# Attention with wider value slots, a ring of 18, a short opening, and the causal mask of the row maxima on VectorE

## The reference

```
scores = einsum('bihd,bjhd->bhij', q, k) * SCALE      # 32 heads, four to a key head
scores = where(causal, scores, finfo.min)
attn = softmax(scores, axis=-1)
out = einsum('bhij,bjhd->bihd', attn, v)
x = layernorm(x + out.reshape(b, s, 1024) @ wo)
```

## Time and profile before

| | us |
|---|---|
| median of 3 runs (3942.48 to 3944.07) | 3943.87 |
| the profiled execution | 3945.43 |
| its span, first to last instruction | 3943.6 |
| PE busy | 3616.7 (92%) |
| VectorE busy | 2041.4 (52%) |
| POOL busy | 1863.9 (47%) |
| ScalarE busy | 1429.3 (36%) |

### The profile page before, as it was taken

The page is one execution under the profiler, slowest core; times in us unless marked ns, Lnnn a source line. Parts: engine busy times, 40 slices in busy tenths (PEclk is TensorE's granted clock), DMA queues, the critical chain, the costliest instruction groups (busy, mean ns, idle before and its releaser), DMA issues. The chain is left out here.

```text
span 3943.6 us, 73049 instructions
## 1 busy us (share of the span) xinstructions
PE 3616.7 (92%) x25741; PEld 2464.1 (62%) x25741; DVE 2041.4 (52%) x3597; ACT 1429.3 (36%) x1821; POOL 1863.9 (47%) x807
## 2 busy tenths in 40 slices
PE   8999989999999989999999999999839999999975
PEld 7888875555555555555555555555428888888851
DVE  3121227566666666666666665666234444443448
ACT  2111103455555555555555554555521111110114
POOL 0000003887797798788789778878910000000000
PEclk9999997999999999999999999999969999999989
DMA  5333333111111111111111111110043232223237
GB/s 187 109 107 121 106 101 82 39 30 45 45 29 48 45 31 36 47 43 26 45 45 31 45 44 36 33 30 10 7 145 87 72 83 80 78 77 80 69 114 248
DMA packets 222653, 269.69 MB, mean 68 GB/s; under 512 B 59608, under 2 KB 145112, under 8 KB 222328
## 3 DMA queue, kind: packets, MB, share of 16 engines
q1 hardware_dynamic: 222328, 265.50, 23.2%
HBM read 167.38 MB, written 97.52 MB: 67 GB/s over the span
## 5 line engine op out<-in xcount | busy, mean ns | idle before, releaser
L716 DVE TENSOR_REDUCE p_part_max<-p_qm 128x1 f32<-128x512 f32 (+3 forms) x2240 | 1411.3, 671 | 792.9 <-PE p_qm L565 543.6
L535 POOL TENSOR_TENSOR p_psums<-p_psums,p_probs 128x1024 f32<-128x1024 f32 x672 | 1595.6, 2374 | 123.7 <-ACT p_probs L675 74.0
L675 ACT ACTIVATE p_probs<-p_km 128x1024 f32<-128x1024 f32 x1024 | 1008.7, 1022 | 770.6 <-PE p_km L589 516.2
L565 PE MATMUL p_qm<-p_k_st,p_q_st 96*128 96x512 f32 (+3 forms) x2560 | 984.9, 432 | 11.1 <-DMA p_q_st<-q_hi 10.7
L589 PE MATMUL p_km<-p_q_st,p_k_st 97*128 97x512 f32 x2048 | 709.1, 426 | 24.7 <-issue 24.7
L32 POOL MEMSET p_ident<- 128x128 f32 x4 | 0.8, 204 | 1511.8 <-POOLq L791 929.8
L565 PEld LDWEIGHTS p_qm<-p_k_st,p_q_st 96*128 96x128 f32 x2560 | 484.6, 200 | 300.3 <-DVE p_part_max L716 164.7
L599 PE MATMUL p_o<-p_probs,p_v 128*32 128x256 f32 (+1 forms) x9216 | 630.5, 382 | 0.2 <-ACT p_probs L672 0.2
L589 PEld LDWEIGHTS p_km<-p_q_st,p_k_st 97*128 97x128 f32 x2048 | 385.4, 199 | 100.1 <-issue 31.5
L599 PEld LDWEIGHTS p_o<-p_probs,p_v 128*32 128x32 f32 x9216 | 244.6, 111 | 269.3 <-issue 144.9
L531 POOL TENSOR_TENSOR p_psums<-p_probs 128x1024 f32<-128x1024 f32 x112 | 266.0, 2375 | 309.9 <-ACT p_probs L675 308.3
(11 more groups left out here) (153 smaller groups left out, 3699.7 us busy)
## 6 DMA issues: line engine op xcount, KB each, us to landing
p_q_st<-q_hi SPq DMA_DIRECT2D x128, 256.0 KB, 4.8
p_x_raw<-in_L_attn_x SPq DMA_DIRECT2D x8, 2048.0 KB, 8.4
q_hi<-p_out_hi SPq DMA_DIRECT2D x64, 256.0 KB, 2.0
q_lo<-p_out_lo SPq DMA_DIRECT2D x64, 256.0 KB, 2.3
p_q_st<-q_lo SPq DMA_DIRECT2D x64, 256.0 KB, 4.4
attended_T<-p_o_raw SPq DMA_DIRECT2D x128, 128.0 KB
p_a_raw<-attended_T SPq DMA_DIRECT2D x32, 512.0 KB, 4.3
p_recip<-reciprocals SPq DMA_DIRECT2D x128, 128.0 KB, 5.9
```

What stands on the lines that cost most here:

```text
L535: pool.tensor_tensor(sums[:, :, :], sums[:, :, :], probs[s % PB][:, :, :], ALU.add).then_inc(added, 1)
L565: last = pe.matmul(bank[:, x * keys:(x + 1) * keys], q_st[par][0:ROWS, c, h + x, sub * P:(sub + 1) * P], k_st[par][0:ROWS, j * CK:j * CK + ...
L675: act.activation(probs[s % PB][:, :, :].rearrange("p h q -> p (h q)"), km[s % 2][:, :, :].rearrange("p a b -> p (a b)"), ACT.Exp, scale=SC ...
L716: dve.reduce_max(part_max[c][:, h:h + heads, sub, j], qm[bank_of(i)][:, 0:item_width(i)].rearrange("p (h k) -> p h k", h=heads), AX.X).the ...
```

## The change

Five edits in `attend`.

1. The values of up to five steps are done together. `SLOTS` cuts each chunk's 2c + 2 steps into equal parts of at most five: 2; 4; 3, 3; 4, 4; 5, 5; 4, 4, 4; 5, 5, 4; and 4, 4, 4, 4. That is 18 slots a group. PE does all scores of a slot, with their items between them, then the values of the slot before. No item is placed behind values any more.
2. The ring `probs` has 18 tiles instead of 12.
3. `POOLED` is 2c - 1 for c > 1 and 0 for chunks 0 and 1.
4. The mask matmuls of the items are gone. For a diagonal item VectorE runs one `tensor_tensor_reduce` per head: it adds `mask_q` (now fp32, 512 wide, zero but for its last 128 columns) to the bank in place and takes the maximum into `part_max`. Ahead of the first stands a semaphore increment, which takes the wait.
5. Ahead of group 0 only items 0 to 15 are done. The other items of group 0, and those it does for group 1, are placed by `OPENING`: 28 in steps 0 to 3, 44 in steps 4 to 17, 56 in steps 18 to 39, 72 in steps 40 to 71. From then on `STEADY` places two a step, and the last group's `CLOSING` its own items only.

```diff
-    PB = 12
+    MOST = 5
+    SLOTS = []
+    for c in range(NC):
+        n = 2 * c + 2
+        parts = -(-n // MOST)
+        cuts = [FIRST_STEP[c] + (n * i + parts - 1) // parts for i in range(parts + 1)]
+        SLOTS += [(c, list(range(a, b))) for a, b in zip(cuts, cuts[1:])]
+    PB = 18
-    POOLED = [2 * c for c in range(NC)]
+    POOLED = [2 * c - 1 if c > 1 else 0 for c in range(NC)]
...
+    ROW_AT = [ITEMS.index(("maxrow", c)) for c in range(NK)]
+    FIRST_AHEAD = ROW_AT[0] + 1
+    STEADY = place([(0, AHEAD), (NS, NI + AHEAD)])
+    OPENING = place([(0, FIRST_AHEAD)] + [(FIRST_STEP[2 * c] - 2, ROW_AT[c] + 1) for c in range(1, NK)]
+                    + [(NS, NI + AHEAD)])
+    CLOSING = [[(ahead, i) for ahead, i in items if not ahead] for items in STEADY]
...
-        mask_q = sb("p2_mask_q", [P, P], BF16)
+        mask_q = sb("p2_mask_q", [P, CK], F32)
...
                 for x in range(item_heads(i)):
                     last = pe.matmul(bank[:, x * keys:(x + 1) * keys], q_st[par][0:ROWS, c, h + x, sub * P:(sub + 1) * P],
-                                     k_st[par][0:ROWS, j * CK:j * CK + keys], start=True, stop=j < c)
-                    if j == c:
-                        last = pe.matmul(bank[:, (x + 1) * keys - P:(x + 1) * keys], ident_bf[:, :], mask_q[:, :],
-                                         start=False, stop=True)
+                                     k_st[par][0:ROWS, j * CK:j * CK + keys], start=True, stop=True)
...
+            def group(n, par, placed):
+                for sl, (_, steps) in enumerate(SLOTS):
+                    for s in steps:
                         scores(n, par, s)
+                        for ahead, i in placed[s]:
+                            item(n + ahead, (par + ahead) % 2, i)
+                    if sl > 0:
+                        values(n, par, sl - 1)
...
-                dve.reduce_max(part_max[c][:, h:h + heads, sub, j], qm[bank_of(i)][:, 0:item_width(i)].rearrange(
-                    "p (h k) -> p h k", h=heads), AX.X).then_inc(item_read, 1)
+                if j < c:
+                    dve.reduce_max(part_max[c][:, h:h + 1, sub, j], qm[bank_of(i)][:, :], AX.X).then_inc(item_read, 1)
+                else:
+                    hold()
+                    keys = item_keys(i)
+                    for x in range(heads):
+                        part = qm[bank_of(i)][:, x * keys:(x + 1) * keys]
+                        last = dve.tensor_tensor_reduce(
+                            part, part, mask_q[:, CK - keys:CK], 1.0, LOWEST, ALU.add, ALU.max, part_max[c][:, h + x, sub, j:j + 1])
+                    last.then_inc(item_read, 1)
```

More of the change, by code:

```diff
@@ L289, in offset @@
         return P if t == 2 * c + 1 else 0
-    POOLED = [2 * c for c in range(NC)]
+    POOLED = [2 * c - 1 if c > 1 else 0 for c in range(NC)]
+    POOL_CHUNKS = [sum(m > 0 for m in POOLED[:c]) for c in range(NC + 1)]
     ADDS_BEFORE = [sum(max(0, m - 1) for m in POOLED[:c]) for c in range(NC + 1)]
@@ L303, in attend @@
     TLAG = 4
+    LOWEST = -3e38
     def key_tiles(c, sub, j):
@@ L349, in attend, with row_steps @@
     bank_user = lambda i: i - QM if i >= QM else max(x for x in range(NI) if x % QM == i) - NI
+    def row_steps(placed):
+        return [(s, ahead, ITEMS[i][1]) for s, items in enumerate(placed) for ahead, i in items
+                if ITEMS[i][0] == "maxrow"]
     def at_least(engine, semaphore, value):
@@ L441, in store_o, with group @@
                              ).then_inc(o_stored[c % 2], 16)
-            def group(n, par, last=False, load=True):
+            def group(n, par, placed, load=True, more=True):
                 b, g = batch_head(n)
@@ L616, in values @@
                 last.then_inc(slot_done, 1)
-                if t == 2 * c + 1 and c > 0:
+                if t == 2 * c + 1 and POOLED[c]:
                     pe.wait_ge(added, n * NADD + ADDS_BEFORE[c + 1])
                     weighted(ones[:, :], psums[c % 2], CQ, 0, False).then_inc(chunk_done, 1)
-            def group(n, par, last=False):
-                done = 0
-                for k, (part, s, _) in enumerate(PARTS):
-                    if part == "scores":
+            def group(n, par, placed):
+                for sl, (_, steps) in enumerate(SLOTS):
+                    for s in steps:
                         scores(n, par, s)
-                    elif s >= 0:
-                        values(n, par, s)
+                        for ahead, i in placed[s]:
+                            item(n + ahead, (par + ahead) % 2, i)
+                    if sl > 0:
+                        values(n, par, sl - 1)
                     elif not (isinstance(n, int) and n == 0):
                         values(n - 1, 1 - par, NSL - 1)
-                    for i in ROUND[done:ITEMS_BY[k]]:
-                        if i >= AHEAD:
-                            item(n, par, i)
-                        elif not last:
-                            item(n + 1, 1 - par, i)
-                    done = ITEMS_BY[k]
             pe.wait_ge(ident_done, 2)
             pe.wait_ge(consts_done, 6)
-            for i in range(AHEAD):
+            for i in range(FIRST_AHEAD):
                 item(0, 0, i)
-            group(0, 0)
+            group(0, 0, OPENING)
             with pe.Fori(0, NG // 2 - 1) as i:
-                group(2 * i + 1, 1)
-                group(2 * i + 2, 0)
-            group(NG - 1, 1, last=True)
+                group(2 * i + 1, 1, STEADY)
+                group(2 * i + 2, 0, STEADY)
+            group(NG - 1, 1, CLOSING)
             values(NG - 1, 1, NSL - 1)
@@ L708, in _, with hold @@
         def _(dve):
+            def hold():
+                dve.sem_inc(held, 1)
             def item(m, i):
@@ L720, in item, with group @@
                     dve.reduce_max(row_max[c][:, :], part_max[c][:, :, :, :].rearrange("p h s j -> p (h s) j"), AX.X).then_inc(max_done, 1)
-            def group(n, last=False):
-                for i in ROUND:
-                    if i >= AHEAD:
-                        item(n, i)
-                    elif not last:
-                        item(n + 1, i)
+            def group(n, placed):
+                for items in placed:
+                    for ahead, i in items:
+                        item(n + ahead, i)
+            dve.wait_ge(consts_done, 4)
             for i in range(2):
                 dve.memset(k_st[i][ROWS:ROWS + 1, :].bitcast(F32), 1.0).then_inc(consts_done, 1)
-            for i in range(AHEAD):
+            for i in range(FIRST_AHEAD):
                 item(0, i)
-            group(0)
+            group(0, OPENING)
             with dve.Fori(0, NG // 2 - 1) as i:
-                group(2 * i + 1)
-                group(2 * i + 2)
-            group(NG - 1, last=True)
+                group(2 * i + 1, STEADY)
+                group(2 * i + 2, STEADY)
+            group(NG - 1, CLOSING)
 class Chain:
```

115 lines of the change are left out of this document (50 added, 65 removed).

## The result

| | us |
|---|---|
| before, median of 3 runs | 3943.87 |
| changed, median of 3 runs (3843.30 to 3849.85) | 3846.84 |
| ratio, with its 95% interval | 0.9755 (0.9732 to 0.9777) |
| the profiled execution (also 3846.84), its span | 3845.1 |
| forecast | 3834 (3775 to 3965) |

The change takes 97 us off. That is the predicted direction, and 13 us above the forecast. First the page of the changed kernel: PE's share and the new instruction of VectorE (count | busy, mean ns of one | idle before).

A forecast was written before the change was run, and what follows sets the result against it. PE was taken to bound groups 1 to 14, VectorE the opening, POOL the last group's second half. Savings of 95 (fourteen groups), 15 (last group) and 0 (opening), 110 us, gave 3835.4, as median 3834 us (3775 to 3965).

The forecast's parts named there:

- Masks off TensorE: PE, each group: removing 64 mask matmuls, sixteen for each width, saves 5.4 us.
- Fewer slots and VectorE: Each group: 36 slots become 18, 4.1 us less; PE waiting for VectorE's reads in scores phases, 9.5 us more.
- the formula: Scores phase of n steps: last item starts at 1.71 + (2n - 4) x 0.61 us, values 0.33 later.
- POOL: Each group: 6.6 us waiting goes except 0.9, 4.1 of clock returns; more steps of ones on PE add 3.0.
- The masked read: VectorE's add-and-maximum instruction: 0.28, 0.41, 0.54, 0.68 us by width, including 0.08 for writing its maximum out.
- rival 3: VectorE becomes the bound, masked reads at half rate: 4039 us; chance 0.13 for beyond 3965.
- The cost of a dearer read: Groups: a dearer masked read delays PE in 90 of 144 places; 0.1 us more per read costs 4.0 us.
- The opening: Before and in group 0: PE starts about 617.7, group 0 takes 154 us, ends at 771.7; net nothing, bounds 12.
- The last group: Paced by POOL's adds in its second half: 130 us against 146, charged as 15 us less.
- Rival 1: The masked read's maximum comes out free and POOL never waits: 3764 us; chance 0.13 for under 3790.
- Rivals 2: The masked read acts as a dear pair, 0.17 us more each, 6.8 a group: 3941 us; chance 0.24 (3885 to 3965).
- Rival 4: Opening: PE stands for the row-maxima copy, inside the forecast; more late copies in group 0, 12 us more; no separate chance.

The follow-up runs named there:

- mask_alone: The kernel before with only the row-maxima mask moved from PE's matmuls to VectorE: 3931.32 us, ratio 0.9966.
- masks_on_pe: The changed kernel with the mask added by PE's bf16 matmuls again and one plain VectorE reduce per bank: 3835.81 us, ratio 0.9728.
- slots_of_two: The changed kernel with slots of at most two steps instead of five, 36 a group: 3892.51 us, ratio 0.9872.
- pool_2c: The changed kernel with POOLED = 2c as before, 49 POOL adds a group instead of 42: 3887.33 us, ratio 0.9854.
- reads_twice: The changed kernel with an unused plain VectorE maximum of the same columns added ahead of every masked read: 4169.96 us, ratio 1.0571.
- long_opening: The changed kernel with all 72 items done ahead of group 0, as in the kernel before: 3825.62 us, ratio 0.9701.
- row_first: The changed kernel with SP issuing the first copy of the row maxima ahead of group 1's loads: 3833.68 us, ratio 0.9718.

## Why the prediction was right, and where not

**Masks off TensorE** (5.4 us a group less) was right for PE's own work and wrong as a gain of the changed kernel. `mask_alone` shows 3.7 to 5.8 us less of scores phases; `masks_on_pe` shows that in the changed kernel the same matmuls fit into PE's waits for VectorE. The forecast did see both, the saving and the waiting it opens, in two terms with opposite signs. What it didn't say is that they cancel. It also left out the stop for the last row maximum, which the edit made 0.6 us longer in every group.

**Fewer slots and VectorE.** The sum of three terms, -5.4 - 4.1 + 9.5, was nothing, and the sum holds: the whole group came within 0.5 us of the forecast. The terms don't, and that the sum does is in part luck. The phases came out longer than the formula, five steps 5.78 for 5.70, four 4.73 for 4.48, three 3.38 for 3.26, and that of steps 34 to 37, where PE stands for the last row maximum, 6.8: 5.4 us a group in all, though VectorE's reads were cheaper than priced. (The formula's 1.71 is also 0.05 above the 0.57 + 0.40 + 0.69 that it is made of.) On the other side, the forecast charged these waits against a PE that had none, and the kernel before had 9.9 us a group of them; a slot of two steps took 2.29 us there and not the 0.95 x 2 + 0.09 = 1.99 of its prices. The waits of the weight loads grew by 6.0 us, from 9.9 to 15.9. And `slots_of_two` shows that 9.5 was booked on the wrong cause: of the waits only 4.8 go with the width. The formula took each place at 0.61 us on the mean; reads are not spread evenly, and the slots with eleven of them in eight items (steps 12 to 15 and 60 to 63) measured 5.24. The values of four steps, 1.87, are the forecast's 4 x 0.43 + 0.14.

**POOL.** 6.6 us a group of waiting were to go but for 0.9, and 4.1 of clock were to come back. All 6.6 went, and the clock rose from 0.96 to 0.98, 5.6 - 0.02 x 133 = 2.9 us. Together 9.5 for a forecast of 9.8, and `pool_2c` brings back wait and clock alike. The forecast's 3.0 for the ones fits `pool_2c` to 1 us. So a group is 3.0 - 9.5 = 6.5 us less by these terms, and 7.2 by the trace; 0.7 stays unplaced.

**The masked read.** Forecast 0.28, 0.41, 0.54, 0.68; measured from start to start behind another masked read 0.25, 0.38, 0.52 and 0.65. A plain reduce would come every 0.20, 0.33, 0.46 and 0.60 us (its duration less the overlap of 0.09). I had added 0.08 for the second part, and it is 0.04 to 0.05 behind a masked read and nothing behind a plain one. The record shows the second part as an instruction of its own, 0.14 us long, which is what the Trainium skill (VectorE: DVE Perf Modes, Two Vector instructions with no wait between them) says of an op that writes out its accumulator: two instructions, here as `CUSTOM_DVE_ANT_0` and `DVE_READ_ACCUMULATOR2_ANT`. That it is two doesn't make it dear, since the next read begins before it has ended. Half rate, rival 3, would be 0.13 us more at 128 columns than a plain reduce and 0.53 at 512, and at both it is 0.05 at most: the price of the rate was the part of the sum that mattered most, and it held. The halved throughput that the Trainium skill gives for two fp32 sources in SBUF (Vector Engine (DVE) Microarchitecture Reference, Points that are easy to get wrong) is neither shown nor refuted, as one source here lies in PSUM.

**The cost of a dearer read.** I had 0.625 of it on the path. `reads_twice` gives 0.88, of which about 0.3 is the clock, and the clock was no part of my figure; 0.55 is left, near what I had.

**The opening is the mis-sized term.** The start was right to 0.7 us (617.7, measured 618.4), and the earlier trace rows did carry the stop. Group 0 was to take 154 us and took 166.8, and group 1 started 16.8 us later than in the kernel before, at an edit put at nothing with bounds of 12 either way. Of this, 3.3 us follow from the forecast's own sum: it has group 0 end at 771.7, and held that against 772.2, a bound 3.8 us behind the first scores of group 1 in the kernel before (768.4). The exponentials of the last steps of chunks 1, 3, 5 and 7 begin at 642.9, 677.7, 724.9 and 782.9, and cut the group in four:

```profile
618.40:642.90 24.50, 23.89 (x55) 13.71 (x56) 19.72 (x53) 4.96 (x6) 0.00 (x0) 0.50 0.00 0
642.90:677.70 34.80, 33.24 (x257) 18.46 (x256) 25.74 (x64) 15.54 (x18) 14.27 (x6) 0.95 0.14 36
677.70:724.90 47.20, 43.79 (x354) 25.07 (x353) 33.90 (x83) 22.96 (x25) 33.25 (x14) 1.00 0.10 24
724.90:782.90 58.00, 54.90 (x446) 31.80 (x446) 42.10 (x121) 31.03 (x35) 47.44 (x21) 1.00 0.11 30
```
| steps | items | forecast | measured | clock |
|---|---|---|---|---|
| 0 to 5 | 35 | 21.9 | 24.5 | 0.50 |
| 6 to 19 | 43 | 29.8 | 34.8 | 0.95 |
| 20 to 41 | 55 | 44.3 | 47.2 | 1.00 |
| 42 to 71 | 67 | 51.6 | 58.0 | 1.00 |
| the tail | | 0 | 2.2 | |

(The forecast's four pieces, 17.6, 30, 45 and 55 us, are shared out here by steps.) The first two stretches cost 7.6 us more, for which the 6 for cold clock and late copies was about right. The other 11.5 us came at full clock. What failed is the price of the dense slots. I had carried 1.72 us a step into steps 40 to 71. The steady groups show just that for two items a step: steps 42 to 71 take 1712.68 - 1660.73 = 51.95 us there, 1.73 each. But group 0 has 67 items in these steps, not 60, and each of the seven more cost 6.0 / 7 = 0.86 us, VectorE's place and some more. The formula had the 0.61 for it; I didn't charge them. `long_opening` gives the edit by itself: group 1 begins at 761.5 with the 72 items ahead, at 785.2 without, 24 us for this edit alone and twice its bounds, of which the other edits win 7 back (768.4 to 761.5). The 21 us for which PE stands for the copy are most of that: `row_first` won 13 of them.

**The last group** was to take 130 and took 133.8, with POOL's 10.4 us where the forecast had put its pace. It was charged 15 us against 146.3, a bound 4.7 us behind the first scores; against 151.0 it gave 17.2.

**The rivals.** Rival 1 had its premises half met, with POOL's wait at zero and the read's second part at 0.05 instead of 0.08, but the longer phases and the opening took what they gave. Rivals 2 and 3 are out by the pitch. Rival 4, 12 us more in group 0, has the size of what came, and a different cause: not late copies, but dense slots. The whole came to 3847 for 3834. Of the 13 us between, the opening made 17 and the part after attention 3, and 1.5 lie between median and profiled execution of the kernel before; groups 1 to 14 and the last one gave 6 and 2 more than forecast. So the forecast lies close partly because misses cancel.

## What to carry to other kernels

When an instruction moves from the binding engine to another, price it at the place where the two meet: the same edit saved 12 us where POOL was late, and cost 11 where VectorE's reads were already the last thing of every phase. Undo edits one by one once the whole is timed, since a net gain of 97 us held two edits that cost 11 and 21. Measure the same mark in both kernels: bounds 4 us apart hid a part of the opening's loss here. And where a phase opens with the other engine idle, hand that engine its first item before anything else: one item a slot, moved, was worth 45 us, as much as the wider slots (46) or POOL's smaller share (40).

## What the runs showed that I had not expected

- PE's clock is 0.61 to 0.62 over the first 36.6 us of group 0 though the records have PE busy for 35.7 of them, with a stop of 21 us ahead or of 3.3. PE is paced by VectorE there and starts 4.7 matmuls a us, where `long_opening` starts 8.5 at a clock of 0.97.
- Taking matmuls out of PE went with a lower clock, 0.96 to 0.93 in `mask_alone`, and giving it more with a higher one, 0.98 to 0.99 in `masks_on_pe`.
- A masked reduction with its accumulator's read keeps the pace of a plain reduce when it stands behind one, 0.21 us from start to start at 128 columns for durations of 0.29. Behind another masked reduction it is 0.04 us longer and comes every 0.25.
- `reads_twice`, in which PE is held by VectorE, ran at 0.93 where the changed kernel ran at 0.98: of the 20.5 us that its group grew some 8 were clock.
